# One fused attention scan and feed-forward kernel: K and V projected three tiles earlier, gate and up weights moved by column quarters

## What is computed

```python
k = x @ Wk.T ; v = x @ Wv.T                  # per head, k then rotated (cos, sin of the position)
def step(W, kv):                             # scan over blocks of 16 tokens, W starts as the identity
    kc, vc = kv
    z = kc @ W
    return W - kc.T @ ((z - vc) * 2.0 / (16 * 32)), z
out = layernorm(z) * ln_gamma + ln_beta
x = layernorm(x + out @ Wo.T)
g = (x @ gate_w.T) * gate_s ; u = (x @ up_w.T) * up_s      # 512 -> 1408, ternary weights
x = layernorm(x + ((silu(g) * u) @ down_w.T) * down_s)
```

## Time and profile before

| | |
|---|---|
| median of 3 runs | 1939.27 us (1938.07 to 1940.27) |
| the profiled execution | 1946.0 us |
| its span | 1944.2 us |
| TensorE busy | 1852.8 us (95%) |
| VectorE busy | 1186.0 us (61%) |
| SyncE's and ScalarE's DMA queues | 46.0% and 2.7% of 16 engines' span |

### The profile page before, as it was taken

One profiled execution on the slowest core, in us unless ns is written; L12 is line 12 of the kernel. 1 busy time (PEld: TensorE's weight loads), 2 busy tenths in 40 slices (PEclk: granted clock), 3 DMA queues, 4 the chain that ended last, 5 costly groups with the idle time before them and its releaser, 6 DMA issues.

```text
span 1944.2 us, 60610 instructions
## 1 busy us (share of the span) xinstructions
PE 1852.8 (95%) x25792; PEld 1478.3 (76%) x25792; DVE 1186.0 (61%) x2612; ACT 547.9 (28%) x1236; POOL 638.4 (33%) x775
## 2 busy tenths in 40 slices
PE   6569999999999999999999999999999999999887
PEld 4348777877877777877777787777878878777676
DVE  3555666666666656666665666666666666666643
ACT  2113222232223232322223232222322232322222
POOL 1113333333333333333333333333333333333333
PEclk9779999999999999999999999999999999999999
DMA  7674554455444455545445545444554544555310
GB/s 265 201 222 134 152 151 129 140 166 165 140 147 147 141 146 162 157 144 155 127 144 161 164 143 159 148 130 141 165 167 139 151 147 137 148 153 150 93 55 23
DMA packets 302512, 287.26 MB, mean 148 GB/s; under 512 B 42784, under 2 KB 252320, under 8 KB 302112
## 3 DMA queue, kind: packets, MB, share of 16 engines
q1 hardware_dynamic: 295968, 265.26, 46.0%
q10 hardware_dynamic: 6272, 18.09, 2.7%
HBM read 152.65 MB, written 139.20 MB: 150 GB/s over the span
## 4 chain that ended last, share of the span: by engine, by line
PE 76%; DVE 9%; DMA 7%; SPq 4%; ACT 2%; issue 2%; ACTq 0%; POOL 0%; POOLq 0%; DVEq 0%
PE gu_acc L787 30%; PE work L768 24%; PE down_acc L799 13%; PE scan_acc L740 4%; PE scan_acc L757 3%; DVE x_tok L956 2%; SPq L306 2%; DMA z_scr<-v_rows 2%; DVE hid L1032 2%; DMA landed<-x1T_scr 2%; DVE turned L961 2%; DVE state L1027 1%; DMA landed<-zT_scr 1%; SPq L350 1%; ACT hid L571 1%
## 5 line engine op out<-in xcount | busy, mean ns | idle before, releaser
L500 POOL TENSOR_TENSOR hid_lo<-hid,hid_hi 128x256 fp32r<-128x256 f32 x352 | 263.0, 747 | 629.9 <-ACT hid_hi L581 629.8
L787 PE MATMUL gu_acc<-x_hi,gw 128*128 128x256 f32 x1372 | 375.2, 306 | 8.7 <-DVE hid L1032 3.2
L571 ACT ACTIVATE hid<-gu_acc,gate_scale 128x256 f32<-128x256 f32 x343 | 162.6, 474 | 765.6 <-PE gu_acc L787 765.4
L1032 DVE SCALAR_TENSOR_TENSOR hid<-gu_acc,up_scale,hid 128x256 f32<-128x256 f32 x343 | 165.5, 483 | 300.5 <-ACT hid L571 300.5
L787 PE MATMUL gu_acc<-x_lo,gw 128*128 128x256 f32 x1372 | 339.5, 280 | 0.0
L787 PE MATMUL gu_acc<-x_hi,uw 128*128 128x256 f32 x1372 | 338.8, 280 | 0.0
L787 PE MATMUL gu_acc<-x_lo,uw 128*128 128x256 f32 x1372 | 338.0, 279 | 0.0
L1027 DVE SCALAR_TENSOR_TENSOR state<-scan_acc,half_step,state 128x256 f32<-128x256 f32 x512 | 223.5, 478 | 170.2 <-PE scan_acc L757 164.9
L787 PEld LDWEIGHTS gu_acc<-x_hi,gw 128*128 128x128 f32 x1372 | 258.0, 188 | 44.9 <-DVE hid L1032 18.7
L799 PE MATMUL down_acc<-dw,hid_hi 128*128 128x512 f32 x704 | 282.0, 401 | 2.4 <-POOL hid_lo L500 2.2
L799 PE MATMUL down_acc<-dw,hid_lo 128*128 128x512 f32 x704 | 279.1, 396 | 0.0
(11 more groups left out here) (121 smaller groups left out, 2230.4 us busy)
## 6 DMA issues: line engine op xcount, KB each, us to landing
x_fm<-xT SPq DMA_DIRECT2D x64, 256.0 KB, 3.4
k_scr<-k_tok SPq DMA_DIRECT2D x32, 512.0 KB, 6.6
k_rows<-k_scr SPq DMA_DIRECT2D x512, 32.0 KB, 2.1
z_scr<-v_rows SPq DMA_DIRECT2D x32, 512.0 KB, 3.5
z_tok<-z_scr SPq DMA_DIRECT2D x512, 32.0 KB, 1.8
x_tok<-x SPq DMA_DIRECT2D x32, 512.0 KB, 5.7
out<-x_tok SPq DMA_DIRECT2D x31, 512.0 KB, 3.4
v_rows<-v_scr SPq DMA_DIRECT2D x488, 32.0 KB, 2.0
```

The source lines that it names most:

```text
L500: pool.tensor_tensor(hid_lo[m % RING][:], hid[m % 2][:], hid_hi[m % RING][:].bitcast(F32), ALU.subtract).then_inc(hid_lo_ready, 1)
L571: act.activation(hid[m % 2][:], gu_bank(n, m)[:, 0:TOK], ACT.Silu, scale=gate_scale[:, m:m + 1]).then_inc(silu_done, 1)
L787: mm = pe.matmul(gu_bank(n, m)[:, k * TOK:(k + 1) * TOK], lhsT=w[:, c, m * P:(m + 1) * P].bitcast(dt), rhs=part[:, c].bitcast(dt), start=( ...
L1032: dve.scalar_tensor_tensor(hid[m % 2][:], gu_bank(n, m)[:, TOK:2 * TOK], up_scale[:, m:m + 1], hid[m % 2][:], ALU.mult, ALU.mult).then_inc ...
```

## The change

- Tick t (from 3 on, `STEADY`) projects tile n = t + 3 (`LEAD` = 3) instead of tile t; scan, O and feed-forward keep their ticks. So ticks -1 to 2 project tiles 0 to 5 and half of 6: eight units in tick 1's slots with 6 matmuls in each slot, four more at the end of its slot 15, six in slots 0 to 5 of tick 2, tile 6's first two in slots 9, 10, 12 and 13. Tick 28 projects half a tile and ticks 29 to 31 none.
- Scratch tensors `k_scr`, `v_scr`, `kT_scr` have one part for each tile. K of odd early tiles lies in `v_tok` and the `hid` buffers, V of the early ones in `x_tok` and `landed`. K is stored in two transfers. Turned K goes by DMA from tile 2 on.
- In ticks 1 and 2 the low part of x is made on GpSimd, and the scaling of Wo by gamma in tick 1 is done on ScalarE instead of VectorE.
- A gate or up piece is a quarter of the columns of all 512 rows, so a row of it is 352 x 4 = 1408 B; each piece is still 704 KB. Copies, loads and weighings are spread anew, all of them earlier.
- Tile 1's V rows are all loaded by SyncE; SyncE's orders for ticks 1 and 2 are written out.
- New waits where a buffer serves twice.

```diff
-WEIGHED = {(1, 13): (0,), (1, 15): (1,), (2, 1): (2,), (2, 3): (3,), (2, 6): (4,), (2, 8): (5,), (2, 10): (6,), (2, 11): (7,),
-           (2, 12): (8,), (2, 13): (9, 10, 11)}
-EARLY_TICKS = 3
-HALF_UNITS = {1: (0, 2), 2: (2, NC)}
+WEIGHED = {(1, 5): (0,), (1, 8): (1,), (1, 11): (2,), (1, 13): (3,), (2, 0): (4,), (2, 2): (5,), (2, 4): (6,), (2, 6): (7,),
+           (2, 9): (8,), (2, 10): (9,), (2, 11): (10,), (2, 13): (11,)}
+STEADY = 3
+LEAD = 3
+FRONT = STEADY + LEAD
+BY_PE = 2
+K, V = 0, 1
+HALVES = ((0, 2), (2, NC))
+FIRST_UNITS = ((K, 1, 1), (V, 1, 1), (K, 2, 0), (V, 2, 0), (K, 2, 1), (V, 2, 1), (K, 3, 0), (V, 3, 0))
+MIDDLE_UNITS = ((K, 3, 1), (V, 3, 1), (K, 4, 0), (V, 4, 0))
+SECOND_UNITS = ((K, 4, 1), (V, 4, 1), (K, 5, 0), (V, 5, 0), (K, 5, 1), (V, 5, 1))
 LAST = NT - 1
-LONE = 1
 ZEROED = 3
 SMALL = 8
 LN_EPS = 1e-5
...
-        PIECES = [(w, c, c + 1) for w in (gw, uw) for c in range(NC)] + [(dw, c, min(c + 3, NM)) for c in range(0, NM, 3)]
+        QUARTER = INTER // NC
+        PIECES = ([w[:, :, c * QUARTER:(c + 1) * QUARTER] for w in (gw, uw) for c in range(NC)]
...
-            return (gu_acc, down_acc[1])[b] if n == 0 else down_acc[0] if n < EARLY_TICKS else work
+            return (gu_acc, down_acc[1])[b] if n == 0 else down_acc[0] if n < FRONT else work
+
+        def k_half(n, b):
+            if n < FRONT and n % 2:
+                return v_tok[:] if b == 0 else hid_both[:].rearrange("p a t -> p (a t)")
+            return k_tok[:, b, :]
+
+        def v_half(n, b):
+            if n == 0 or n >= FRONT:
+                return (v_tok, k_sin)[b][:]
+            if n % 2:
+                return landed[:].rearrange("p h g t -> p (h g t)")[:, b * DM:(b + 1) * DM]
+            return x_tok[:, b, :]
 
         def k_by_dma(n):
-            return n >= EARLY_TICKS
+            return n >= BY_PE
 
...
             def store_v(n, b):
                 sp.wait_ge(v_ready, 2 * n + b + 1)
-                if b == 0 and n >= 1:
-                    sp.wait_ge(rows_in[0], 256 * n)
-                    sp.wait_ge(rows_in[1], 256 * n)
-                sp.dma_start(v_scr[b], v_tok[b][:]).then_inc(v_stored, 16)
+                if b == 0:
+                    sp.wait_ge(v_stored, 32 * n)
+                sp.dma_start(v_scr[n, b], v_half(n, b)).then_inc(v_stored, 16)
 
             def store_k(n):
-                sp.wait_ge(k_ready, 2 * n + 2)
-                sp.dma_start(k_scr.rearrange("b t f -> t b f"), k_tok[:]).then_inc(k_stored, 16)
+                sp.wait_ge(k_stored, 32 * n)
+                for b in range(BATCH):
+                    sp.wait_ge(k_ready, 2 * n + b + 1)
+                    sp.dma_start(k_scr[n, b], k_half(n, b)).then_inc(k_stored, 16)
 
             def store_turned(scr, stored):
...
+                elif t == 1:
+                    store_v(1, 0)
+                    store_k(1)
+                    store_v(1, 1)
+                    load_x_fm(3)
+                    store_z(0, 0, NS // 2)
+                    load_k_half0(1)
+                    load_z(0, 0, NS // 2, 16)
+                    store_v(2, 0)
+                    load_v_half0(1, 0)
+                    load_v_half0(1, 1)
+                    store_k(2)
+                    store_z(0, NS // 2, NS - 1)
+                    store_v(2, 1)
+                    load_x_fm(4)
+                    load_z(0, NS // 2, NS - 1, 32)
+                    store_kT(2)
+                    store_z(0, NS - 1, NS)
+                    load_z(0, NS - 1, NS, 48)
+                elif t == 2:
+                    load_k_half1(1)
+                    load_v_half1(1)
+                    store_v(3, 0)
+                    store_k(3)
+                    store_v(3, 1)
+                    load_x_fm(5)
+                    store_v(4, 0)
+                    store_kT(3)
+                    store_k(4)
+                    store_v(4, 1)
+                    load_kT(2)
+                    load_x_fm(6)
+                    load_x(0)
+                    store_v(5, 0)
+                    store_kT(4)
+                    store_k(5)
+                    store_z(1, 0, NS // 2)
+                    store_v(5, 1)
+                    load_k_half0(2)
+                    load_z(1, 0, NS // 2, 16)
+                    store_kT(5)
+                    load_v_half0(2, 0)
+                    load_v_half0(2, 1)
+                    load_x_fm(7)
+                    store_z(1, NS // 2, NS - 1)
+                    load_z(1, NS // 2, NS - 1, 32)
+                    store_z(1, NS - 1, NS)
+                    load_z(1, NS - 1, NS, 48)
+                else:
...
+            def low_x(n, b):
+                pool.wait_ge(x_high, 2 * n + b + 1)
+                pool.tensor_tensor(fm[1][:, :, b, :], x_fm[:, :, b, :], fm[0][:, :, b, :].bitcast(F32),
+                                   ALU.subtract).then_inc(x_low, 1)
...
+            def scale_wo(c):
+                act.wait_ge(small_in, 16 * SMALL)
+                w = x1_tok[c // 2][:, c % 2, :]
+                act.activation(w, w, ACT.Copy, scale=ln_gamma[:, c:c + 1]).then_inc(wo_scaled, 1)
...
+                elif m == 0:
+                    act.wait_ge(k_stored, 32 * FRONT)
+                    act.wait_ge(k_turned, 2 * FRONT)
...
-            def ffn_piece(i, c):
-                return (c, c + 1) if i < 2 else (3 * c, min(3 * c + 3, NM))
+            def ffn_piece(w, i, c):
+                w = w.rearrange("(c p) n -> p c n", p=P)
+                return w[:, :, c * QUARTER:(c + 1) * QUARTER] if i < 2 else w[:, 3 * c:min(3 * c + 3, NM), :]
 
             def copy_ffn(i, c):
                 dst, src = ((gw_scr, gwT), (uw_scr, uwT), (dw_scr, dwT))[i]
-                c0, c1 = ffn_piece(i, c)
-                act.dma_start(dst[c0 * P:c1 * P].rearrange("(c p) n -> p c n", p=P),
-                              src[c0 * P:c1 * P].rearrange("(c p) n -> p c n", p=P)).then_inc(ffn_copied[i][c], 16)
+                act.dma_start(ffn_piece(dst, i, c), ffn_piece(src, i, c)).then_inc(ffn_copied[i][c], 16)
 
             def load_ffn(i, c):
-                dst, src = ((gw, gw_scr), (uw, uw_scr), (dw, dw_scr))[i]
-                c0, c1 = ffn_piece(i, c)
+                src = (gw_scr, uw_scr, dw_scr)[i]
                 act.wait_ge(ffn_copied[i][c], 16)
-                act.dma_start(dst[:, c0:c1].bitcast(F32), src[c0 * P:c1 * P].rearrange("(c p) n -> p c n", p=P)
-                              ).then_inc(ffn_in[i][c], 16)
+                act.dma_start(PIECES[i * NC + c].bitcast(F32), ffn_piece(src, i, c)).then_inc(ffn_in[i][c], 16)
 
             act.wait_ge(wk_in, 16 * NC)
             for c in range(NC):
...
+                    if t == 1 and s == 0:
+                        load_ffn(0, 0)
+                        copy_ffn(1, 0)
+                    if t == 1 and s == 2:
+                        load_ffn(0, 1)
+                    if t == 1 and s == 4:
+                        copy_ffn(1, 1)
+                    if t == 1 and s == 6:
+                        load_ffn(0, 2)
+                        copy_ffn(1, 2)
+                    if t == 1 and s == 8:
+                        load_ffn(0, 3)
+                    if t == 1 and s == 10:
+                        load_ffn(1, 0)
+                        copy_ffn(1, 3)
                     if t == 1 and s == 12:
-                        load_v_rows(1, 0)
-                    if t == 2 and s in (0, 2, 4, 6):
-                        copy_ffn(2, s // 2)
-                    if t == 2 and s in (1, 3, 5, 7):
-                        load_ffn(1, s // 2)
-                    if t == 2 and s in (8, 9, 10, 11):
-                        load_ffn(2, s - 8)
+                        load_ffn(1, 1)
+                        copy_ffn(2, 0)
+                    if t == 1 and s == 14:
+                        copy_ffn(2, 1)
+                    if t == 1 and s == 15:
+                        load_ffn(1, 2)
+                        copy_ffn(2, 2)
+                    if t == 2 and s == 0:
+                        load_ffn(1, 3)
+                    if t == 2 and s == 1:
+                        copy_ffn(2, 3)
+                    if t == 2 and s == 2:
+                        load_ffn(2, 0)
+                    if t == 2 and s == 4:
+                        load_ffn(2, 1)
+                    if t == 2 and s == 6:
+                        load_ffn(2, 2)
+                    if t == 2 and s == 7:
+                        load_ffn(2, 3)
...
             def project_k(n, b, c0, c1):
                 if c0 == 0:
                     pe.wait_ge(x_low, 2 * n + b + 1)
-                    if 1 <= n < EARLY_TICKS:
+                    if 1 <= n < FRONT:
                         pe.wait_ge(k_mul, 6 * n + 3 * b)
                     elif b == 1 and n >= 1:
                         pe.wait_ge(v_ready, 2 * n + 1)
                     elif n >= 1:
-                        pe.wait_ge(o_added, 2 * (n - 2))
+                        pe.wait_ge(o_added, 2 * (n - 2 - LEAD))
```

(63 more changed lines are left out.)

423 lines of the change are left out of this document (256 added, 167 removed).

## The result

The changed kernel takes 1948.3 us in the median (1947.4 to 1949.5, 5 runs), the kernel before 1938.8 beside it (1934.6 to 1940.3, 5 runs): a ratio of 1.0053 [1.0038, 1.0067], slower by half a per cent. The forecast was 1929.2, faster, and the range ended at 1946. The profiled execution of the changed kernel took 1948.8, close to its median; the one of before, 1946.0, stood 6.7 above the median of its first three runs (7.2 above 1938.8).

What follows compares the result with a forecast made beforehand. TensorE was taken to bound the steady ticks (56.8 of 57.0 us busy), with free time in the opening. End -10.6, front +2, half a unit -1.5, steady 0: -10.1 on the 1939.3 median gives 1929.2 us, range 1908 to 1946.

Steps and rivals of the forecast that it cites:

- The front: Opening ticks 1 and 2 up to the first gate matmul: gate start at 144, +2 us, bounds 128 and 162.
- 142 at 0.92: Opening: 98.7 us of DMA work in 107.7, a share of 0.92, would leave the gate start at 142.
- Ten us of waits there are likely: SyncE's order in ticks 1 and 2: loads standing behind others were to cost about ten us of waits.
- the waits that leave: Opening: waits expected to go, among them late down-weight weighings; 4 us less from second O addition to gate start.
- The price of small rows: Gate and up weights in 1408 B rows: 0 to 5.4 us more DMA engine time, 2 taken.
- Half a unit between the gates: After the gate start in tick 2: 6 projection matmuls no longer stand between gates, -1.5 us.
- The steady ticks: Ticks 3 to 28: same work, order and banks per tick, so 0 us, from -4 to +3.
- The end: Ticks 28 to 31: 227.9 to 217.3 us, -10.6, with ticks 29 to 31 at 53.8 each; bounds -14.8 and -4.3.
- The DMA engines fill up: Rival, chance 0.16: opening stays at DMA share 0.8, gate start 157 to 162, time 1944, slower.
- The end gives nothing: Rival, chance 0.14: tick 31's waits repeat in ticks 29 to 31, 55.9 each, -4.3 us, time 1935.5.
- The front gets faster: Rival, chance 0.20: small rows end the longest waits in the opening, gate start near 130, time 1915.
- The signs named: Profile readings for gate start, opening busy shares, z store landing, steady and last ticks, listed beforehand as what would show the forecast.

Runs made afterwards that it cites:

- e14: Changed kernel with tiles 4's and 5's x loaded early, tile 4's V in another buffer and residual x issued behind tile 3's stores: ratio 0.9994.
- e1: Changed kernel with tile 5's x loaded ahead of tick 1's last z load: ratio 1.0029.
- e13: Changed kernel with tiles 4's and 5's x loaded early and the residual x moved forward two places on SyncE: ratio 0.9990.
- e18: e14 run again unchanged, on the chip of e17: ratio 1.0012, median 1941.9 us.
- e4: Kernel before with only the gate and up weights cut into column quarters (rows of 1408 B): ratio 0.9985.
- e2: Changed kernel with gate and up weights back in blocks of 128 rows (rows of 5632 B): ratio 1.0078, 1955.9 us.
- e5: Kernel before, unchanged, profiled a second time (one run): span 1941.5 us.
- e17: e14 with 8 filler matmuls on constant weights in each of both stands of ticks 29 to 32: ratio 0.9978, median 1935.4 us.
- e8: e1 with 1 matmul instead of 12 in each moved unit of tiles 3 to 5, 132 left out: ratio 1.0018.

## Why the prediction was wrong

**The front, +2 us forecast, +13.2 measured: the step that failed.** Its two sums were right. The DMA engines moved 30.92 MB for 23.95, 7.0 more (forecast 7.3), and were busy for 0.80 of 122.1 us, 98 (forecast 98.7). PE was busy for 92.5 us (forecast 98.0). Neither sum set the gate start. It is made of a tail of 22 us, in which the engines have little to move (share 0.39) and VectorE is busy for 17.6, and of the chain that ends in the O addition. Spreading 98.7 us over the whole stretch, tail included, gave 142 at 0.92; but the tail takes only some 9 of them, so the other 90 would have had to fit into the 86 us ahead of it, a share of 1.05. e14, the fullest, moved its 95 us with 0.96 to 1.03 ahead of the tail. So 142 was a bound that could hardly be met, before any wait was counted.

The sentence that failed is the next one: "Ten us of waits there are likely" on SyncE's order, named with both loads that turned out to be late (tile 5's x behind 16 row loads, the residual x behind tile 4's stores), and then set off against "the waits that leave". These ten are what came: e1 took off 7.7 by the first load, e13 and e14 another 3.8 by the second. Single profiles scatter by some 3 us, but the ratios, 10 us in all from the changed kernel to e14 and e18, bear the sum out. Of the credits the tail came at half its size, 2.1 us of 4, and the quarters gave 2.9 us by e4's ratio in the kernel before; neither was there to cover these waits.

**The price of small rows.** The weights' queue took 45.7 us for 14.75 MB in the opening after (37.4% of 122.1), 45.0 for 14.98 MB before (41.7% of 108.0): 3.10 and 3.01 us per MB, so 1.0 on 11.5 MB. But these two kernels differ in more than the cut. The pairs that differ in it alone are e2 and the changed kernel, and before and e4; the weights' queue in the openings of e2 and e4:

```profile
q10 hardware_dynamic: 4794, 14.65, 36.0%
q10 hardware_dynamic: 10506, 14.92, 48.7%
```

Of 119.7 and 98.3 us that is 2.94 us per MB in e2 for 3.10 in the changed kernel, and 3.21 in e4 for 3.01 in before and 3.08 in e5: 0.13 to 0.20 more, 1.5 to 2.3 us on 11.5 MB, where one kernel alone scatters by some 0.1 per MB. The forecast had 0 to 5.4 and took 2. The Trainium skill (DMA: Bandwidth & Descriptors, "Why small descriptors are slow (HBM only)") has a fixed cost for each packet, from which the forecast estimated 2.3 us for rows of 1408 B and 0.6 for those of 5632 B, 1.7 for the step; these pairs agree as far as their scatter lets one see. What the Trainium skill (DMA: Bandwidth & Descriptors, "Queues, rings and completion order") says of a whole packet drained at a time, which made a faster front a rival, fits e4: the gates at 132.4, as that rival's near 130, though without the lead. That this rule is the cause isn't shown.

**Half a unit between the gates, -1.5 us.** It didn't show: from the gate start to tick 3 it took 9.5 us for 8.2. PE was busy for 8.8 of the 9.5 us, at a clock of 0.55, with 77 matmuls; in before for all 8.2, at 0.82, with 82. So there were fewer matmuls, and the clock took the gain. The term had no clock in it.

**The steady ticks, 0.** Right: 57.15 for 57.23 in the mean, -2.2 in all, in the bounds.

**The end, -10.6 us forecast, -7.7 in this profile, -4.9 in the mean of twelve.** Right in mechanism, wrong in size: the second term that failed. It was taken from tick 32, whose one profile had a clock of 1.00: 45.8 us of PE and 6.6 of waits, with 1.4 more for the row loads 53.8. Ticks 29 to 31 took 55.4 in the mean. About 0.7 of the missing 1.6 is in the waits even at the full clock: the two ticks that kept it took 54.5 and 54.6, with 8.6 us of waits. Another 0.6 is the eight ticks in which the clock stayed low behind the stand of slot 14, at some 2.7 us each; tick 31's 0.97 in before gave a hint of it. The rest, 0.3 us, is the ordinary ticks at 0.94. Tick 28 took 56.4 for 55.9. With filler in the stands the four ticks take 214.7, below the forecast 217.3.

**The sum.** Medians: 1938.8 + 14.5 (tick 3's start) - 4.9 = 1948.4; 1948.3 was measured. That exactness is luck. The 14.5 comes from one profile each, and the sum leaves out the steady ticks and what stands behind tick 32, which were 2.2 us shorter each in this pair.

**The rivals.** "The DMA engines fill up" (0.16) gave 157 to 162 and 1944. Its share of 0.80 is the one measured, and its side is the one that came; but the cause was for the larger part two places in SyncE's order, and 5.8 MB less gave 6.7 us with the order as it was and 1.5 to 2.7 with the order mended. This rival is nearer than the forecast in both numbers, 155.2 and 1948.3, and the kernel came out slower still than it said. "The end gives nothing" stood at -4.3, nearer to the mean of -4.9 than the forecast. "The front gets faster" held for the quarters alone.

**The signs named.** The first gate matmul at 137 to 151: missed (155.2). PE over 0.85 busy in ticks 1 and 2: missed (0.76). DMA at 0.85 or more: missed over the whole (0.80), met in the first two windows. A z store landing under 6 us: 5.3 and 6.5 for the smaller ones, but 8.6 in the median of the two half tiles, missed. Steady ticks at 57.0: met. Ticks 29 to 31 at 53 to 54.5: 54.8, 54.8, 54.3, with PE at 47.2 to 48.5 and not 45.8.

## What to carry to other kernels

When work is moved into a stretch whose engines have room, don't stop at the sums of busy time: follow the in-order queue that issues the loads, call by call, and give each load that now stands behind others its lateness; a wait that the working finds there is a cost until another wait is shown to cover it. Compute a share only up to the transfer on which the tail hangs, and add the tail. And where work is taken off TensorE but a wait stays, the tick is not worth its matmuls at the full clock: take its length from several profiles of a like tick, waits included. Filling such a lull with cheap matmuls paid 6.5 us of the median here, where taking the work out had brought 4.9 us in its ticks.

## What the runs showed of the hardware

A stand of 2.3 us in an otherwise busy stretch was followed, in most ticks but not in all, by some us at a granted clock of 0.50 to 0.66; with 16 added matmuls of 0.26 us a tick it stayed at 1.00, and three ticks were 7.6 us shorter (e17, e18, one profile each). A drop of some 4 us changed the length of a tick by under 1 us, one of some 10 us by about 3. Leaving 132 matmuls out of the opening gave nothing (e8), with PE busy for 13.8 of 46 us and the clock at 0.51. And the DMA engines held 337 and 347 GB/s over 30 and 20 us with both queues loaded (e14), where the densest window of before showed 278.
